# Moving each head's maximum into the queries with one VectorE addition, in place of a ScalarE copy and four transfers

## What is computed

```
q = x @ Wq ; k = ctx @ Wk ; v = ctx @ Wv           # 20 heads of 8 channels
s = q_h @ k_h.T * scale                            # 128 rows x 77 tokens per head
p = softmax(s)                                     # over groups of tokens
x = (p @ v) @ Wout + bias + x                      # next layer
```

## Time and profile before

| | |
|---|---|
| median of 3 runs | 2385.61 us (2381.63 to 2386.51) |
| profiled execution | 2388.74 us, span 2386.9 us |
| busy share of the span | TensorE 93%, VectorE 59%, ScalarE 45%, GpSimd 18% |
| mean granted TensorE clock | 0.974 |
| transfers of `move_top` | 768 (192 steps, four each) |

### The profile page before, as it was taken

How to read it: one execution, slowest core, us unless ns; L and a number is a source line. 1 busy time by engine, 2 the same in 40 slices (tenths; PEclk the granted TensorE clock), 3 DMA queues, 4 the chain that set the end, 5 groups by cost and what they waited for, 6 DMA issues and landing times.

```text
span 2386.9 us, 75525 instructions
## 1 busy us (share of the span) xinstructions
PE 2215.2 (93%) x26880; PEld 1843.4 (77%) x26880; DVE 1411.6 (59%) x4319; ACT 1079.7 (45%) x2689; POOL 436.8 (18%) x847
## 2 busy tenths in 40 slices
PE   1699999999999999999999999999999999999976
PEld 1577887888788788878878887888888788888865
DVE  3236666566566566656656665665665566666654
ACT  0244444444444444544544454454444444445431
POOL 0112112212121121211212121122122121212110
PEclk9799999999999999999999999999999999999985
DMA  2111111111111111111111111111111111111000
GB/s 83 49 45 34 47 47 33 45 46 42 36 47 41 36 47 47 36 42 47 41 37 47 42 35 48 42 38 44 46 37 40 46 42 36 47 47 32 26 7 5
DMA packets 69396, 97.64 MB, mean 41 GB/s; under 512 B 19805, under 2 KB 45613, under 8 KB 69006
## 3 DMA queue, kind: packets, MB, share of 16 engines
q1 hardware_dynamic: 67328, 89.15, 13.2%
q10 hardware_dynamic: 1678, 3.33, 0.5%
HBM read 30.59 MB, written 5.24 MB: 15 GB/s over the span
## 4 chain that ended last, share of the span: by engine, by line
PE 77%; DVE 13%; issue 6%; SPq 1%; DMA 1%; DVEq 1%; ACTq 1%; ACT 0%
PE ps_c L745 10%; PE ps_s L633 9%; PE ps_c L678 8%; PE ps_s L606 8%; PE ps_q L587 7%; PE ps_k L698 5%; PE ps_k L527 4%; DVE top L956 4%; PE ps_s L650 4%; PE ps_k L542 4%; PE ps_k L703 3%; PE ps_c L733 3%; PE ps_k L553 2%; PE ps_c L711 2%; PE ps_k L572 2%
## 5 line engine op out<-in xcount | busy, mean ns | idle before, releaser
L956 DVE TENSOR_REDUCE top<-ps_s 128x6 f32<-128x462 f32 (+3 forms) x1024 | 512.3, 543 | 174.6 <-PE ps_s L606 174.3
L1173 POOL TENSOR_TENSOR k_blocks<-k_sb,mask_k 128x231 f32<-128x231 f32 x512 | 282.8, 574 | 810.3 <-PE ps_s L633 795.7
L856 ACT ACTIVATE p_t<-ps_s 116x512 f32<-116x512 f32 (+1 forms) x768 | 369.0, 545 | 70.7 <-PE ps_s L633 70.5
L1001 DVE TENSOR_TENSOR weighted<-ps_k,probs 128x462 f32<-128x462 f32 (+1 forms) x256 | 143.1, 559 | 318.3 <-PE ps_k L703 313.6
L678 PE MATMUL ps_c<-p_t,v_rows 116*27 116x128 f32 (+1 forms) x7168 | 282.6, 280 | 14.0 <-DMA v_rows<-v_img 11.5
L606 PE MATMUL ps_s<-k_blocks,q_sb 32*128 32x231 f32 (+1 forms) x3584 | 274.4, 375 | 16.5 <-issue 15.8
L745 PE MATMUL ps_c<-o_t,wo 128*80 128x128 f32 x2048 | 275.1, 278 | 0.5 <-ACT o_t L884 0.5
L678 PEld LDWEIGHTS ps_c<-p_t,v_rows 116*27 116x27 f32 (+1 forms) x7168 | 210.6, 107 | 83.8 <-issue 48.5
L633 PE MATMUL ps_s<-q_sb,k_blocks 32*116 32x128 f32 (+1 forms) x5376 | 230.6, 286 | 21.5 <-DMA q_sb<-top_t 12.6
L884 ACT ACTIVATE o_t<-ps_c 80x256 f32<-80x256 f32 x256 | 97.3, 380 | 324.1 <-PE ps_c L733 232.8
L745 PEld LDWEIGHTS ps_c<-o_t,wo 128*80 128x80 f32 x2048 | 231.0, 151 | 14.2 <-issue 13.2
(11 more groups left out here) (106 smaller groups left out, 2969.1 us busy)
## 6 DMA issues: line engine op xcount, KB each, us to landing
v_rows<-v_img SPq DMA_DIRECT2D x128, 227.4 KB
context<-in_ctx SPq DMA_DIRECT2D x64, 336.0 KB, 3.0
q_sb<-top_t SPq DMA_DIRECT2D x576, 6.0 KB
v_rows<-v_img SPq DMA_DIRECT2D x64, 115.2 KB
v_rows<-v_img SPq DMA_DIRECT2D x64, 112.2 KB
x_in<-in_x SPq DMA_DIRECT2D x64, 80.0 KB, 1.9
out_x<-x_out SPq DMA_DIRECT2D x64, 80.0 KB, 1.7
q_sb<-top_t SPq DMA_DIRECT2D x192, 2.0 KB
```

The costliest lines, as they stand in the source:

```text
L856: act.activation(to, source, ACT.Exp, scale=SCALE).then_inc(p_ready, 1)
L956: dve.tensor_reduce(top[c % 2][:, z * BH:z * BH + m], s.rearrange("p (h t) -> p h t", t=T)[:, :, 0:n], AX.X, ALU.max).then_inc(s_top, 1)
L1001: dve.tensor_tensor(weighted[:, lo * T:hi * T], ps_k[:, 0:(hi - lo) * T], probs[:, lo * T:hi * T], ALU.mult).then_inc(w_ready, 1)
L1173: pool.tensor_tensor(k_blocks[c % 3][:, j * GT:(j + 1) * GT].rearrange("p (h t) -> p h t", t=T), k_sb[l][b // 2 % 3][:, at:at + T].unsquee ...
```

## The change

`top` becomes 128 by 128, cleared at the start, and the four maxima instructions write straight to the columns where the heads belong (`top_at`). The transpose L664 therefore loads 128 columns and not 20, and leaves a full 128-partition result in `ps_q`, with zeros wherever a partition holds queries. VectorE then adds this result to both halves of `q_sb` in one instruction (`add_top`). ScalarE's copy, `top_t`, the four transfers and their three semaphores are gone. Whoever waited for the copy or the transfers waits for `top_added`.

```
-        top = [sb(f"top{i}", [128, H]) for i in range(2)]
-        top_t = sb("top_t", [H, S])
+        top = [sb(f"top{i}", [128, 128]) for i in range(2)]
...
-            def move_top(k, c):
-
-                sp.wait_ge(top_evac, raised(k, topped, c))
-                for z in range(4):
-                    lo, m = QUAD * z + GD, heads_in(z)
-                    sp.dma_start(q_sb[c % 3][lo:lo + m, :].rearrange("p (j n) -> p j n", j=2),
-                                 top_t[BH * z:BH * z + m, :].unsqueeze(1).to_broadcast([m, 2, S]))\
-                      .then_inc(top_ready[c % 3], 16)
...
-                if topped(t):
-                    move_top(k, t)
...
-                pe.wait_ge(top_ready[c % 3], raised(k, TOPPED_IN[c % 3], c, per=64, first=0))
+                pe.wait_ge(top_added, raised(k, topped, c))
...
-                pe.wait_ge(top_evac, raised(k, topped, c - 1))
-                pe.transpose(ps_q[0:H, 2 * S:3 * S], top[c % 2][:, :], ident[:, :]).then_inc(top_psum, 1)
+                pe.wait_ge(top_added, raised(k, topped, c - 1))
+                pe.transpose(ps_q[:, 2 * S:3 * S], top[c % 2][:, :], ident[:, :]).then_inc(top_psum, 1)
...
-                act.activation(top_t[:, :], ps_q[0:H, 2 * S:3 * S], ACT.Copy).then_inc(top_evac, 1)
...
+            def top_at(c, z):
+
+
+                lo = QUAD * z + GD
+                return top[c % 2][:, lo:lo + heads_in(z)]
+
+            def add_top(k, c):
+
+
+                dve.wait_ge(top_psum, raised(k, topped, c))
+                q = q_sb[c % 3][:, :].rearrange("p (j n) -> p j n", j=2)
+                m = ps_q[:, 2 * S:3 * S].unsqueeze(1).to_broadcast([128, 2, S])
+                dve.tensor_tensor(q, q, m, ALU.add).then_inc(top_added, 1)
...
                 if e_waves(t):
                     weigh(k, t, 0)
+                if topped(t):
+                    add_top(k, t)
                 if ip(t - 5):
                     norms(k, t - 5)
                     image_branch(k, t - 5, 1, 8)
```

More of the change, by code:

```diff
@@ L188, in e_waves @@
     return ip(wave_step(t))
-def topped_in(i):
-    return lambda c: topped(c) and c % 3 == i
-TOPPED_IN = [topped_in(i) for i in range(3)]
 def build(nc, a):
@@ L338, in build @@
         top_psum = sem("top_psum")
-        top_evac = sem("top_evac")
-        top_ready = [sem(f"top_ready{i}") for i in range(3)]
+        top_added = sem("top_added")
         x_exp = sem("x_exp")
@@ L371, in build @@
                   sum_ready, q_psum, q_evac, s_psum, s_top,
-                  s_sub, top_psum, top_evac, x_exp, p_clear, e_psum, p_ready, u_psum, u_evac, ut_psum, r_ready,
+                  s_sub, top_psum, top_added, x_exp, p_clear, e_psum, p_ready, u_psum, u_evac, ut_psum, r_ready,
                   den_ready, o_ready, ot_psum, ot_evac, y_psum, x_ready, w_psum, w_ready, w_folded, qn_ready, ip_step,
@@ L578, in queries @@
                 pe.wait_ge(q_evac, raised(k, exists, c - 1))
-                pe.wait_ge(top_evac, raised(k, topped, c - 2))
+                pe.wait_ge(top_added, raised(k, topped, c - 2))
                 if l == 0:
@@ L896, in step @@
                     products(k, t - 2)
-                if topped(t):
-                    tops(k, t)
                 if ip(t):
@@ L955, in top_of @@
                     dve.wait_ge(top_psum, raised(k, topped, c - 2))
-                dve.tensor_reduce(top[c % 2][:, z * BH:z * BH + m], s.rearrange("p (h t) -> p h t", t=T)[:, :, 0:n],
+                dve.tensor_reduce(top_at(c, z), s.rearrange("p (h t) -> p h t", t=T)[:, :, 0:n],
                                   AX.X, ALU.max).then_inc(s_top, 1)
@@ L971, in less_top @@
                 dve.tensor_tensor(p[:, :, 0:TXT], s[:, :, 0:TXT],
-                                  top[c % 2][:, z * BH:z * BH + m].unsqueeze(2).to_broadcast([128, m, TXT]),
+                                  top_at(c, z).unsqueeze(2).to_broadcast([128, m, TXT]),
                                   ALU.subtract).then_inc(s_sub, 1)
```

## The result

The changed kernel is slower. Its median is 2411.38 us (2408.22 to 2419.78, four runs) against 2384.9 for the kernel before in the same job (2381.63 to 2386.51, four runs). Its profiled execution took 2411.01 us, with a span of 2409.2, 22.3 us over that of before.

The account below looks back on a forecast made before the run. TensorE held 77% of the chain, VectorE 13%; transfers were waited for only at start-up, and VectorE's chain from L1110 set the loop. -24.2 + 13.0 + 4.2 + 1.8 = -5.2 us gave 2380.4 us, range 2370 to 2394.

Parts of the forecast that it names:

- Start-up, -24.2: While the pipeline fills: removed transfer waits and less half clock gain 24.2 us, between 18 and 31.
- the first step's numbers: First program step: values' product L678 starts at about 58.6; 6.2 of 9.65 us of waits go, 3.4 stay.
- no half clock at the two later places: Start-up, sign of being right: no half clock around 117 to 124 and 151 to 155.
- the waits for transfers: Start-up: of TensorE's 24.1 us waiting for maxima's and values' transfers, 19.7 us are gained.
- the clock (forecast 4.5): Start-up: less matmul at half clock gains 4.5 us, between nothing and 11.4.
- The addition, 0.42 us, 0.04 after the transpose: VectorE's new addition takes 0.42 us and starts 0.04 us after transpose L664 ends.
- The rival that VectorE pays for its holds: Loop, addition and norms: semaphore holds cost VectorE 0.17 each, 0.58 lost a period, 2398.7 us; slower case's chance 0.18.
- The delay of 1.00 and the cover of 0.76: Loop, layer-0 position: norms start 1.00 us later; VectorE's idle 0.69 plus 0.07 of overlap covers 0.76.
- So 0.24 us goes through to L1110: Loop, layer-0 position: delay beyond the cover reaches L1110 and the chain's end, 0.24 us in 54 periods, 13.0 us.
- Behind the loop, 0.84 a period: Five written-out periods after the loop: nothing covers the addition, 0.84 us each, 4.2 us lost.
- The weight load: Transpose loading 128 columns instead of 20: 0.03 us more at each layer-1 position, 59 times, 1.8 us.

Follow-up runs that it names:

- mark_hold: The changed kernel with GpSimd held from its marking (L1149) on until VectorE's small instructions of both groups are through: 2371.83 us.
- wait_only: The kernel before with only VectorE's wait for the transpose added ahead of the norms at the layer-0 position: 2419.81 us.

## Why the prediction was wrong

The forecast was 2380.4 us in a range of 2370 to 2394; the time is 2411.4, outside it. By the steps of the prediction:

- **Start-up, -24.2.** Right: 23.8, with the first step's numbers close (values' product at 58.47, forecast 58.6; a wait of 4.0 left, forecast 3.4) and no half clock at the two later places. By its terms: the waits for transfers fell by 20.1, while, up to the first norms, that for the maxima grew from 6.6 to 7.5 and one of 0.5 for the addition is new, so 18.7 (forecast 19.7). That leaves some 5 for the clock (forecast 4.5); TensorE had 9.3 us of matmul at half clock instead of 22.9, which allows at most 6.8.
- **The addition, 0.42 us, 0.04 after the transpose.** Right in size (416 ns on average); it starts 0.03 after the end of the 0.30 us transpose. The rival that VectorE pays for its holds had the sign, but not the mechanism: this start shows no such price, and `mark_hold`, which has the same holds, loses only 0.24. The price itself was misread: in the loop L664 has no idle time before it in the earlier trace rows, because TensorE's L678 ran from 1216.28 to 1217.35. It stood behind TensorE's own work, not behind a hold.
- **The delay of 1.00 and the cover of 0.76.** Both right: the norms start 0.67 after the transpose starts instead of 0.31 before it, 0.98 later.
- **"So 0.24 us goes through to L1110", times 54.** This is the step that failed. It took the durations between the norms and L1110 as fixed. They are not: the delayed instructions meet GpSimd's and grow by 0.72. Then 0.98 + 0.72 - 0.76 = 0.94 goes through, and 0.95 was measured. Over the 54 periods the loss is 45.0 us where the prediction had 13.0.
- **Behind the loop, 0.84 a period.** Under by the same cause. There two of the instructions were already lengthened before the change, so less was added: from the norms to L1110 it was 2.86 us, in the changed kernel 3.04 (2187.66 to 2190.70). The 0.84 and this 0.18 make 1.02, and the transposes are that much further apart (8.39 instead of 7.37).
- **The weight load.** A median of 138 ns, against 89 with 20 columns (in `wait_only`). That `mark_hold` loses just 0.24 leaves nothing above the 0.03 given to it.

The span's account, by VectorE's norms. The first come at 199.40 before and 175.61 after; those of the first written-out period at 2096.26 and 2117.50, so the loop's 54 periods are 45.0 us longer. Three written-out periods on, at 2198.20 and 2222.81, 3.4 more have come. From there to the last norms, at 2373.09 and 2395.42, the changed kernel takes 2.3 less, with a mean granted clock of 0.88 against 0.84. So -23.8 + 45.0 + 3.4 - 2.3 = +22.3, the difference of the spans.

The 45.0 are 0.83 a period, less than the 0.95 of the period shown. Part of that is the clock: in the loop the kernel before runs six stretches of 3.4 us at half clock, TensorE busy throughout, the changed one three. The first of each kernel, before and after:

```profile
407.30:410.70 3.40, 3.40 (x26) 2.56 (x23) 2.73 (x6) 0.58 (x2) 0.00 (x0) 0.50 0.02 5
```

```profile
386.50:389.90 3.40, 3.40 (x22) 2.81 (x22) 1.29 (x3) 0.38 (x1) 0.00 (x0) 0.50 0.48 132
```

What a stretch costs can be read from the loop's turns of six periods, counted from the fourth norms of a turn to the fourth of the next (303.43 to 1992.42 before, 281.89 to 2010.73 after). Before, two turns without such a stretch take 210.38 and 210.43 us, the six with one 211.18 to 211.52. After, five without take 215.47 to 215.84, the three with one 216.55 to 217.04. So a stretch costs about 1.0 to 1.2 us, not the 1.7 that half of its matmul would be, and three fewer, at these prices, give back some 2.3. Without them a turn is 5.3 us longer, 0.88 a period, and 54 x 0.88 - 2.3 = 45.2. Why there are fewer stretches, and where a period gets the last 0.07 between 0.95 and 0.88 back, was not tested.

The trace of before had the warning, next to a row that I quoted. In the written-out period of the earlier trace rows, VectorE of the kernel before:

```profile
2166.30 0.33 DVE L1066 TENSOR_TENSOR rs_u<-rs_t,rs_y 128x24 f32<-128x24 f32 x1
2166.66 0.50 DVE L1068 SCALAR_TENSOR_TENSOR rs_y<-rs_u,rs_y 128x24 f32<-128x24 f32 x1
```

and GpSimd of the kernel before at that time:

```profile
2166.27 0.32 POOL L1163 TENSOR_TENSOR probs<-ones 128x80 f32<-128x80 f32 x1 [5.90 <-PE ps_s L650]
2166.55 1.11 POOL L1173 TENSOR_TENSOR k_blocks<-k_sb,mask_k 128x231 f32<-128x231 f32 x2
```

I had noted that nothing covered there, and not asked why the same instructions took 0.47 us longer than in the loop. Had I, the loop's period would have read: small instructions end at 1219.54, GpSimd's k_blocks begin at 1219.69, and a delay over 0.15 us brings them together.

## What to carry to other kernels

When work is put ahead of a chain of short VectorE instructions, the idle time behind them is only half of the question: look also at what GpSimd runs in the time that they are pushed into, and whether any of them already takes two or three times as long elsewhere in the same trace. New work goes into the idle time itself, not ahead of what comes before it; with the addition in one place the change cost 26 us, with the addition a few calls later it gained 23. Where a transfer is late, look first at what stands ahead of it in its queue: here exchanging two calls gave 16 us, 11 of them in the start-up.

## What the runs showed of the hardware

VectorE's 24-column instructions from SBUF to SBUF took 0.18 us alone and up to 0.50 beside GpSimd's 231-column multiplications of 0.55 us each, int32 with one input as well as float32 with two, while GpSimd's kept their length (1.10 to 1.12 for the two). VectorE's instructions with an input in PSUM that met them in the rows read here were not lengthened. L1110 at 2167.10 lies wholly beside GpSimd's second multiplication (about 2167.10 to 2167.66) and took 0.42 us, as without it; the four maxima that lie over the whole pair in `mark_hold` (1165.49 to 1167.45) took 1.96 us together, as in the changed kernel, where GpSimd is idle at that point (1187.96 to 1189.92).
